# Loading the heads of two attentions quad by quad, and the weight subtractions of the second close behind its inputs

## The reference

```
x = layernorm(x + linear_attention(x))     # phi = exp(x omega - |x|^2/2), 128 features
x = layernorm(x + attention(x, memory))    # softmax, causal, keys and values led by the memory
x = layernorm(x + moe(x))                  # 16 experts of 128, top 4 of 2 groups, 2 shared
# linear attention: S = cumsum(phi_k v), Z = cumsum(phi_k)
# y = phi_q S / (phi_q Z + EPS); then y @ W_proj + b_proj
```

## Time and profile before

| | us |
|---|---|
| median of 3 runs | 2217.79 (2216.48 to 2221.77) |
| profiled execution, time | 2214.3 |
| its span | 2212.2 |
| first load of the linear attention issued | 130.98 |
| its first matmul, its first exponential | 175.31, 198.13 |
| first load of the softmax attention issued | 730.11 |
| its first product, its first exponential | 769.57, 833.78 |
| second close, GpSimd's first subtraction | 1454.70 |

### The profile page before, as it was taken

The page is one execution under the profiler, slowest core; times in us unless marked ns, Lnnn a source line. Parts: engine busy times, 40 slices in busy tenths (PEclk is TensorE's granted clock), DMA queues, the critical chain, the costliest instruction groups (busy, mean ns, idle before and its releaser), DMA issues. The chain is left out here.

```text
span 2212.2 us, 38875 instructions
## 1 busy us (share of the span) xinstructions
PE 1867.3 (84%) x13696; PEld 1218.1 (55%) x13696; DVE 1486.7 (67%) x3864; ACT 912.7 (41%) x1398; POOL 389.1 (18%) x511
## 2 busy tenths in 40 slices
PE   7914999999688058989989999956689999999997
PEld 4603766767455013333333333324478888888886
DVE  7921554555598167888878888523498877777776
ACT  5602554555233005656656666721333233323322
POOL 2110212110332501111111111255220000000000
PEclk9966999999899558999999999978899999999999
DMA  6961554543388410221222120336500000000000
GB/s 171 222 136 62 121 104 109 111 108 111 116 224 203 113 64 18 74 71 59 73 73 63 62 84 32 110 114 206 162 23 29 30 1 30 29 14 17 20 10 10
DMA packets 167359, 187.39 MB, mean 85 GB/s; under 512 B 80816, under 2 KB 137536, under 8 KB 161044
## 3 DMA queue, kind: packets, MB, share of 16 engines
q1 hardware_dynamic: 131456, 136.45, 21.4%
q0 software_dynamic: 18976, 28.01, 6.7%
q10 hardware_dynamic: 16756, 20.56, 3.5%
HBM read 114.33 MB, written 70.20 MB: 83 GB/s over the span
## 5 line engine op out<-in xcount | busy, mean ns | idle before, releaser
L1402 ACT ACTIVATE sa_prob<-sa_ps_s 128x1024 f32<-128x1024 f32 (+3 forms) x480 | 376.3, 825 | 337.2 <-PE sa_ps_s L1310 194.0
L1460 DVE CUSTOM_DVE_ANT_0 sa_ps_m<-sa_ps_m,sa_later 128x282 f32<-128x282 f32 (+4 forms) x640 | 278.5, 461 | 102.7 <-PE sa_ps_m L1283 101.4
L1463 DVE TENSOR_REDUCE sa_piece_max<-sa_ps_m 128x1 f32<-128x512 f32 x384 | 259.2, 688 | 36.6 <-PE sa_ps_m L1283 36.1
L1283 PE MATMUL sa_ps_m<-sa_k,sa_q 96*128 96x358 bf16 (+7 forms) x1024 | 259.4, 304 | 8.7 <-DVE sa_piece_max L1460 6.9
L1801 DVE SCALAR_TENSOR_TENSOR mo_acc<-mo_ps_o,mo_keep,mo_acc 128x256 f32<-128x256 f32 x512 | 212.2, 477 | 71.5 <-PE mo_ps_o L216 71.3
L1438 POOL TENSOR_SCALAR_AFFINE_SELECT sa_prob<-sa_prob 128x256 f32<-128x256 f32 x256 | 102.5, 406 | 579.6 <-ACT sa_prob L1402 576.7
L686 DVE TENSOR_TENSOR la_att<-la_ps_att,la_cap 128x512 f32<-128x512 f32 x128 | 88.3, 690 | 171.6 <-PE la_ps_att L587 171.6
L1667 ACT ACTIVATE mo_h_hi<-mo_h 128x512 fp32r<-128x512 f32 x144 | 91.0, 632 | 272.6 <-DVE mo_h L1783 270.4
L1281 PEld LDWEIGHTS sa_ps_m<-sa_km,sa_q 96*128 96x128 bf16 x512 | 50.7, 99 | 240.6 <-issue 146.6
L1281 PE MATMUL sa_ps_m<-sa_km,sa_q 96*128 96x154 bf16 x512 | 122.9, 245 | 70.3 <-DMA sa_q<-s_q_parts 51.2
L1310 PE MATMUL sa_ps_s<-sa_q,sa_k 99*128 99x512 bf16 (+3 forms) x768 | 180.4, 331 | 2.1 <-ACT sa_prob L1402 2.0
(11 more groups left out here) (197 smaller groups left out, 3835.7 us busy)
## 6 DMA issues: line engine op xcount, KB each, us to landing
s_y<-la_y SPq DMA_DIRECT2D x16, 512.0 KB, 2.9
s_x<-cl_xn SPq DMA_DIRECT2D x16, 512.0 KB, 6.1
s_y<-sa_y SPq DMA_DIRECT2D x16, 512.0 KB, 2.7
mw_raw<-experts SPq DMA_DIRECT2D x18, 384.0 KB, 4.5
s_q_parts<-pj_parts SPq DMA_DIRECT2D x16, 384.0 KB, 5.2
s_k_parts<-pj_parts SPq DMA_DIRECT2D x16, 384.0 KB, 2.6
s_q_parts<-cl_parts SPq DMA_DIRECT2D x16, 384.0 KB, 7.8
s_k_parts<-cl_parts SPq DMA_DIRECT2D x16, 384.0 KB, 6.8
```

The costliest lines, as they stand in the source:

```text
L1283: last = nc.tensor.matmul(ps_m[:, s, a - lo:hi - lo], qs, k[g][0:STACK, j, a - MEM:hi - MEM], start=lo > 0, stop=True, skip_group_check=True)
L1402: nc.scalar.activation(dst, src, ACT.Exp, scale=HD ** -0.5).then_inc(expd[s], 1)
L1460: nc.vector.tensor_tensor_reduce(ps_m[:, s, 0:hi - lo], ps_m[:, s, 0:hi - lo], later[:, BANK + lo - first:BANK + hi - first], 1.0, -BIG, A ...
L1463: nc.vector.tensor_reduce(piece_max[:, j, t, n:n + 1], ps_m[:, s, 0:hi - lo], AX.X, ALU.max).then_inc(piece_done[s], 1)
```

## The change

In the linear attention GpSimd loads quads 1 to 3 of the first round whole, nine transfers each, after `landed[0]` says that q and k of quad 0 are there. SyncE loads only q of quad 0 and, behind it, identity and caps; ScalarE only k of quad 0. In the softmax attention each of the three queues waits for quad g - 1 before it loads quad g, and k of quads 2 and 3 goes from ScalarE to SyncE. In the second close GpSimd's six subtractions go from the stage's start to behind the inputs, one to each; the loop over batch rows is written out in both closes.

```diff
-        POOL_FIRST = [1, 1, 5, 5]
+        POOL_FIRST = [1, 9, 9, 9]
...
             load_stacks(sp, q, "q_parts", 0, 0, 0, landed)
-            load_stacks(sp, q, "q_parts", 0, 0, 1, landed)
+            sp.dma_start(ident[:, :], io["ident"]).then_inc(consts_in, 16)
+            sp.dma_start(cap[:, :, :], io["cap"]).then_inc(consts_in, 16)
...
             load_v(pool, 0, 0)
-            load_v(pool, 0, 1)
-            for pr in range(2, SLOTS):
-                load_stacks(pool, q, "q_parts", 0, 0, pr, pool_landed)
-                load_v(pool, 0, pr)
-            for kk in range(1, ROUNDS):
+            pool.wait_ge(landed[0], 16 * (LOADS - POOL_FIRST[0]) + START)
+            for kk in range(ROUNDS):
                 for pr in range(SLOTS):
-                    pool.wait_ge(y_done[pr], kk * BLOCKS + START)
+                    if not kk and not pr:
+                        continue
+                    if kk:
+                        pool.wait_ge(y_done[pr], kk * BLOCKS + START)
                     load_stacks(pool, q, "q_parts", 0, kk, pr, pool_landed)
                     load_stacks(pool, k, "k_parts", 1, kk, pr, pool_landed)
                     load_v(pool, kk, pr)
...
             load_stacks(act, k, "k_parts", 1, 0, 0, landed)
-            act.dma_start(cap[:, :, :], io["cap"]).then_inc(consts_in, 16)
-            act.dma_start(ident[:, :], io["ident"]).then_inc(consts_in, 16)
-            for pr in range(1, SLOTS):
-                load_stacks(act, k, "k_parts", 1, 0, pr, landed)
...
-            if not on:
-                for e in range(W_SLOTS):
-                    weights.remainder(pool, e)
...
-            with pool.Fori(0, B - 1) as b:
+            for b in range(B - 1):
                 root(b, AHEAD % 2)
                 inputs(b + 1, 0)
+                if not on:
+                    weights.remainder(pool, 2 * b)
                 root(*((b + 1, 0) if on else (b, 1)))
                 inputs(b + 1, 1)
+                if not on:
+                    weights.remainder(pool, 2 * b + 1)
...
-            for g in range(QUADS):
+            load_q(sp, 0, 0)
+            for g in range(1, QUADS):
+                sp.wait_ge(landed[g - 1], 16 * HARD_FIRST + START)
+                sp.wait_ge(pool_landed[g - 1], 16 * (LOADS - HARD_FIRST))
                 load_q(sp, 0, g)
+                if g > 1:
+                    load_k(sp, 0, g)
             maxima(0, 0)
...
-            for g in range(QUADS):
-                load_k(act, 0, g)
+            load_k(act, 0, 0)
+            act.wait_ge(landed[0], 16 * HARD_FIRST + START)
+            load_k(act, 0, 1)
...
-            for g in range(QUADS):
-                load_rest(pool, 0, g, pool_landed)
+            load_rest(pool, 0, 0, pool_landed)
             for i in range(SLOTS):
+                if i:
+                    pool.wait_ge(landed[i - 1], 16 * HARD_FIRST + START)
+                    load_rest(pool, 0, i, pool_landed)
```

More of the change, by code:

```diff
@@ L563, in features @@
                 if c == 0:
-                    pe.wait_ge(landed[pr], 16 * (LOADS - POOL_FIRST[pr]) + START)
+                    if pr == 0:
+                        pe.wait_ge(landed[pr], 16 * (LOADS - POOL_FIRST[pr]) + START)
                     pe.wait_ge(pool_landed[pr], kk * (16 * LOADS) + 16 * POOL_FIRST[pr])
```

## The result

The changed kernel takes 2183.19 us (median of 4 runs, 2179.63 to 2186.68) against 2218.57 before: ratio 0.9838, interval 0.9821 to 0.9854. That is 35.4 us less, and 7 us above the 2176 predicted. Its profiled execution has a span of 2184.6 us, 27.6 less than the one before.

What follows compares the result with a forecast made beforehand. Bound by loads and their issuing in both attention heads, and by subtractions opening the second close; -39.6 + 3 - 5.3 = -42 from 2214.3 gives 2172.4, plus 3.5 for the median 2176 us, range 2161 to 2192.

Steps and rivals of the forecast that it cites:

- Linear head: Linear attention's head: quad 0 lands in 25.5 us, first exponential at 158.5 instead of 198.13; term -39.6 us (-44 to -30).
- rival C: Linear attention: GpSimd's three quads share the engines and come late; +12 us, 2188 us; chance 0.12.
- Softmax head: Softmax attention's head: four-stage chain, first product 13 us earlier, first exponential 3 us later; term +3 us (-11 to +9).
- 731.0 + 4 x 25.5 = 833.0, three handovers of 0.5 us: Softmax head: four stages of 25.5 us plus handovers, with 1 us for the maxima giving 835.5, exponential about 836.4.
- the upper bound of 27: Time to load one quad, read from a single full load by one queue: 26.5 to 27 us; 25.5 taken.
- a sign that it is wrong: Both heads: prediction wrong if quad 0 takes much over 26 us or softmax stages differ from 25.5 by more than 2.
- rival D: Both heads: all loads of a stage meet on two low engines, stages 27 us and more; 2185 us; chance 0.06.
- hidden in GpSimd's waits: Softmax head: GpSimd's clears, the longest 3.51 us, fall into its waits for the next quad.
- Second close: Second close: inputs start 10.6 us earlier, subtractions give back 5.3 us; term -5.3 us (-10.6 to 0).
- each has three subtractions: 3 x 1.77 = 5.3: Second close: each half's chain has three subtractions of 1.77 us between inputs and root, giving back 5.3 us.

Runs made afterwards that it cites:

- e1: Kernel before with only the linear attention's part of the change: 2180.97 us, ratio 0.9831 to the kernel before.
- e4: Changed kernel without the softmax head's waits for the previous quad, k of quads 2 and 3 still on SyncE: 2177.48 us, ratio 0.9811.
- e8: Changed kernel with stacks of q, k, omega and memory keys loaded as six 16-row transfers instead of three: 2132.64 us, ratio 0.9617.
- e5: Changed kernel with SyncE issuing the softmax maxima of quad 0 ahead of its wait for quad 2: 2164.31 us, ratio 0.9744.
- e2: Kernel before with only the softmax attention's part of the change: 2232.90 us, ratio 1.0067 to the kernel before.
- e7: Kernel before with stacks of q, k, omega and memory keys loaded as six 16-row transfers instead of three: 2164.23 us, ratio 0.9751.
- e3: Kernel before with only the second close's part, loops of both closes written out: 2209.26 us, ratio 0.9960 to the kernel before.
- e10: Kernel of e5 with GpSimd's clears of all four slots ahead of its waits for quads 0 to 2: 2150.10 us, ratio 0.9681.
- e12: Kernel before with the change's linear attention and closes parts, without its softmax attention part: 2173.10 us, ratio 0.9786.
- e9: Changed kernel with each of the second close's six subtractions done twice: 2190.37 us, ratio 0.9859 to the kernel before.
- e6: Changed kernel with each of the second close's six subtractions moved ahead of the next inputs: 2186.64 us, ratio 0.9852.
- e11: Kernel of e8 with quad 0's maxima ahead of the wait for quad 2 and GpSimd's clears ahead of its waits: 2119.32 us, ratio 0.9549.

## Why the prediction was right, and where it was off

**Right in sign and range; 7 us too low.** Against its own profiled execution the sum said -42 and the span gave -27.6. Of the 14.4 us between, the softmax head is 8.9, the linear head 2.7; 4.6 lie in stretches costed at 0, and 1.9 went the other way. The medians came out better than the profiled pair, 35.4 us.

**Linear head: right.** The issue of later loads no longer holds ScalarE, quad 0 lands without the others, and no DMA is waited for before quads 1 to 3 (rival C did not come). e1 shows that this part is the whole gain. Its 36.9 us split by the rows: from the first load to TensorE's first product 29.6 us instead of 44.3, 14.7 less; from there to the exponential 0.65 instead of 22.8, 22.2 less, which was ScalarE's issuing. No run leaves GpSimd's wait out of the linear attention, so how much of the 14.7 is the wait and how much the shorter queues is not shown. The term was mis-sized by the stage: 29.1 us to landing instead of 25.5, which e1 repeats with its head of 29.5 us.

**Softmax head: right mechanism, wrong size, and this is the step that failed:** "731.0 + 4 x 25.5 = 833.0, three handovers of 0.5 us". The stages took 29.7, 27.5, 28.3 and 29.4 us, together 114.9. The first of these begins with ScalarE's load, 0.9 us ahead of SyncE's, where the sum began, and the last holds the 1 us that the sum gave to the maxima; without both it is 113.0 instead of 103.5. Two faults lie in it. A handover costs 2.3 us by e4, not 0.5: three of them are 5.4 us of the 9.5. And without these the loading itself took 28.8, 25.2, 26.0 and 26.1 us, 26.5 in the mean and not 25.5: the other 4.1. Most of that is the first stage, and quad 0 of the linear attention, at 29.1 us, had the same; both are above the upper bound of 27 that I read in the earlier trace rows. Why a first stage is longer was not tried. The prediction had named this as a sign that it is wrong, quad 0 much over 26 us or stages more than 2 us off 25.5, and the sign came: 29.1 us, and three of the four stages at 28.3 to 29.7. That the total still came within 7 us of the forecast owes something to luck: the medians fell by 7.8 us more than the two profiled spans. The Trainium skill (DMA: Bandwidth & Descriptors, "Latency and other measured facts") gives about 2 us as the fixed cost of a DMA. The prediction set that beside the sum; e4's 2.3 us a handover is near it.

So the time is near that of rival D (2185, stages of 27 us and more), though its cause was only half there. That the long part of a stage runs on two engines is read from its share, and that the shape does it is shown by e8. That GpSimd's rows meet on the same two engines is not shown; right behind a handover the share is 0.67 and 0.68, so part of the bytes goes by other engines. The Trainium skill (DMA: Bandwidth & Descriptors, "Why a DMA increments its semaphore by 16 and not by 1") has the rule for SP and ACT that a DMA uses as many engines, up to 16, as divide the slowest dimension on both sides; e8's shares of 0.97 to 1.02 with 16 rows agree with it.

**What I had not seen at all:** TensorE's first score needs GpSimd's clears of all four slots. I had called them hidden in GpSimd's waits, and they are, but what waits for them is TensorE. In the changed kernel it cost nothing, in e5 some 8 us.

**Second close: right in sign, the size within the noise of one trace.** In the four kernels without the edit (before, e1, e2, e7) the close takes 115.1, 120.5, 122.6 and 120.4 us; in the eight with it and nothing else there (changed, e3 to e5, e8, e10 to e12) 107.2 to 113.7, 110.2 in the mean. The edit is worth 9.5 us by these means and 8.9 by the ratio of e3, nearer to all of the 10.6 than to the 5.3 I took. The step "each has three subtractions: 3 x 1.77 = 5.3" counted them in full. e3 bears out a third of it (10.6 - 8.9 = 1.7 us); e9, with as many again, cost 3.5 us in the close and 4.7 to 7.2 in the whole, which does not exclude the 5.3; e6 got nothing back. What a subtraction costs there stays open.

## What to carry to other kernels

Making the queues wait until the first block of data has landed brings that block sooner: the softmax attention's first product came 29.5 us after the first load with the waits and 37.7 without (e4). It pays where the first block is all that the compute needs, and an engine that computes should not issue the later blocks at all: in the linear attention that was 22 of the 37 us. Where something small must still pass through that queue before the compute can go on, the staged loads delay it: place the small transfer first, and ask for every semaphore of the first consumer which other engine raises it, and what that engine now waits for. Before ordering transfers at all, look at the DMA share: 0.13 says two engines, and here a different shape (e8) was worth more than the whole order.

## What the runs showed of the hardware

- Three transfers of 8 KB each, on the same queue: two landed in about 2 us and one took 20 to 27 us while loads of quads that used two engines at the end were ahead (before, e5, e10). With 16-row loads ahead all three took 10.6 to 11.1 us (e8), and with none ahead 2.0 to 2.6 us (e11).
- An engine's rate fell when all were busy: two engines moved 53 GB/s (share 0.13), some 26 GB/s each; sixteen moved 136 to 141 with 16-row transfers (e8, over 15 us each, share 0.97 to 1.02), some 9 GB/s each; a share of 0.78 moved 146 in the kernel before. A full share is not a full rate.
- When each quad's load waits for the one before, the engines move 8 to 20 GB/s for 2 us at the handover (windows above); by e4 a handover costs 2.3 us or more.
- The second close took between 115.1 and 122.6 us in four kernels that have the same code there (before, e1, e2, e7): a single profile does not settle a term of 5 us there.
